# Reordering the opening of a two-block attention kernel: two issuing queues, inputs by pairs, weight splits four units later

## The reference

```python
# block 0, NH = 8 heads of 16 channels, x is (16, 128, 256), mask is (16, 256)
q = transpose(x) @ Wq.T                      # q serves as query, key and value
scores = 0.25 * einsum('bhqd,bhkd->bhqk', qh, qh)
logits = (scores * cmask + (1 - cmask) * -1e30) * rmask
x = x + transpose(softmax(logits) @ qh @ Wo.T)
# block 1: adaLN with cond (timestep_embed @ ada_w + ada_b), 16 heads of 128,
# x = x + gate1 * attention(ln(x)...),  x = x + gate2 * ffn(ln(x)...)
```

## Time and profile before

| | us |
|---|---|
| median of 3 runs | 842.45 (839.59 to 842.97) |
| the profiled execution, its time | 839.47 |
| its span, first to last instruction | 837.7 |
| PE busy | 778.3 (93%) |
| DVE busy | 389.4 (46%) |
| ACT busy | 434.5 (52%) |
| POOL busy | 144.7 (17%) |

### The profile page before, as it was taken

The page is one execution under the profiler, slowest core; times in us unless marked ns, Lnnn a source line. Parts: engine busy times, 40 slices in busy tenths (PEclk is TensorE's granted clock), DMA queues, the critical chain, the costliest instruction groups (busy, mean ns, idle before and its releaser), DMA issues. The chain is left out here.

```text
span 837.7 us, 13230 instructions
## 1 busy us (share of the span) xinstructions
PE 778.3 (93%) x4989; PEld 642.0 (77%) x4989; DVE 389.4 (46%) x782; ACT 434.5 (52%) x1189; POOL 144.7 (17%) x136
## 2 busy tenths in 40 slices
PE   4599999985999999999999999999999999799997
PEld 3455555553888888888888898888898888677775
DVE  1156666664234434444554443544543435436443
ACT  1056766663456544536555446465444475475553
POOL 3134343100222111101101011011011132200000
PEclk9999999997899999999999999999999999989999
DMA  6998999700311000000000000000000001030001
GB/s 197 242 167 195 194 188 199 124 8 32 108 39 38 1 1 1 1 2 1 1 1 1 0 0 0 0 0 0 1 2 1 13 27 38 13 101 27 15 10 50
DMA packets 26449, 42.64 MB, mean 51 GB/s; under 512 B 1960, under 2 KB 13728, under 8 KB 26400
## 3 DMA queue, kind: packets, MB, share of 16 engines
q1 hardware_dynamic: 26400, 41.98, 21.4%
HBM read 31.45 MB, written 10.52 MB: 50 GB/s over the span
## 5 line engine op out<-in xcount | busy, mean ns | idle before, releaser
L928 ACT ACTIVATE probs<-pair,nm 128x128 f32<-128x128 f32 x256 | 90.5, 366 | 218.0 <-DVE nm L1015 218.0
L1071 POOL TENSOR_TENSOR probs<-probs,rinv 128x512 f32<-128x512 f32 x64 | 66.6, 1041 | 391.4 <-DVE rinv L1024 391.4
L674 PE MATMUL bank<-x1h,w_hi 128*128 128x512 f32 x256 | 112.2, 438 | 5.0 <-DVE x1l L1001 5.0
L604 DVE TENSOR_REDUCE mx<-ring 128x2 fp32r<-128x512 f32 x128 | 80.1, 684 | 63.9 <-PE ring L403 63.9
L674 PE MATMUL bank<-x1h,w_lo 128*128 128x512 f32 x256 | 101.6, 397 | 0.0
L674 PE MATMUL bank<-x1l,w_hi 128*128 128x512 f32 x256 | 101.5, 397 | 0.0
L541 ACT ACTIVATE pt<-ring 128x512 f32<-128x512 f32 x128 | 70.0, 594 | 43.9 <-PE ring L415 43.9
L1045 DVE COPY Vv<-pair 128x512 f32<-128x512 f32 x64 | 44.3, 692 | 82.8 <-PE pair L674 82.8
L674 PE MATMUL pair<-w_hi,x1l 128*128 128x256 f32 x256 | 72.8, 284 | 0.0
L674 PE MATMUL pair<-w_lo,x1h 128*128 128x256 f32 x256 | 72.7, 284 | 0.0
L674 PE MATMUL pair<-w_hi,x1h 128*128 128x256 f32 x256 | 72.3, 282 | 0.0
(11 more groups left out here) (166 smaller groups left out, 1565.5 us busy)
## 6 DMA issues: line engine op xcount, KB each, us to landing
QS<-qd SPq DMA_DIRECT2D x16, 384.0 KB
stage<-in_L_cond_qkv_w_dram SPq DMA_DIRECT2D x12, 512.0 KB, 7.3
qd<-qh SPq DMA_DIRECT2D x16, 256.0 KB
KS<-qd SPq DMA_DIRECT2D x16, 256.0 KB
mb<-in_cond_dram SPq DMA_DIRECT2D x8, 256.0 KB, 10.2
qd<-ql SPq DMA_DIRECT2D x8, 256.0 KB
KS<-qd SPq DMA_DIRECT2D x16, 128.0 KB
kept<-X SPq DMA_DIRECT2D x1, 2048.0 KB, 8.0
```

The costliest lines, as they stand in the source:

```text
L604: dve.tensor_reduce(mx[:, 2 * b + s, :], ring[:, 2 * b + s, :].rearrange("p (k q) -> p k q", k=2), AX_X, ALU.max, negate=True).then_inc(dv ...
L674: last = nc.tensor.matmul(bank, w(k), x(k), start=(start and i == 0), stop=(stop and i == len(terms) - 1))
L928: last = nc.scalar.activation(probs[:, h % 2, b, :], Sb[:, b * T:(b + 1) * T], ACT.Exp, bias=nm[:, h % 2, b:b + 1], accum_out=sums[:, h % ...
L1071: pool.tensor_tensor(probs[:, h % 2, :, :], probs[:, h % 2, :, :], rinv[:, h % 2, :, None].to_broadcast([P, GB, T]), ALU.mult).then_inc(po ...
```

## The change

- **Two queues for the early loads.** SP keeps x and mask of group 0, Wq and the constants. ACT's stream now begins with eleven transfers: cond, Wo, x and mask of group 1, two of ada_w, and five biases.
- **x in pairs.** `pair(eng, g)` loads x and mask of one group; the single load of groups 2 to 7 goes away. SP issues pair(2) before the loop and pair(g+3) in it.
- **Mask rows first.** DVE makes `rows` in place of POOL; SP waits for their store and issues the four mask-row transfers ahead of gather(0). `spread` is cut in two functions, `mask_rows` and `spread`.
- **First spread in halves.** Group 0's q rows go as two sets of six transfers, for units 0 and 1, then 2 and 3; s(0) waits for the first set, s(2) for the second.
- **Splits four units later.** Half i of the weights is split in unit n = i + 4 on ACT and POOL. `weights(c)` and its wait are as they were.
- **Modulations first.** All four parts stand before the loop.

```diff
+    SPLIT0 = 4
...
-                def spread(g):
+                def mask_rows(g, landed):
...
-                sp.dma_start(X[:, 0:2, :], x[0:2].rearrange("b p d -> p b d")).then_inc(l_x0, 16)
-                mask(0)
+                pair(sp, 0)
                 sp.dma_start(wqo[:, 0, :], Wq).then_inc(l_w, 16)
                 sp.dma_start(cst[:, :], consts).then_inc(l_cst, 16)
...
-                sp.wait_ge(pool_nb, 1)
+                sp.wait_ge(dve_rows, 1)
                 sp.dma_start(rowd.rearrange("t b d -> b t d"), rows[:, :, :]).then_inc(l_nb, 16)
+                sp.wait_ge(l_nb, 16)
+                mask_rows(0, l_head)
                 gather(0)
...
-                sp.wait_ge(l_nb, 16)
-                spread(0)
-                sp.dma_start(X[:, 4:B, :], x[4:B].rearrange("b p d -> p b d")).then_inc(l_x, 16)
-                mask(2)
+                spread(0, slice(0, 2), l_head)
+                spread(0, slice(2, 4), l_q[0])
                 gather(1)
+                pool_free(2)
+                pair(sp, 2)
                 weights(0)
                 weights(1)
                 for g in range(NGR):
                     if g + 1 < NGR:
-                        spread(g + 1)
+                        mask_rows(g + 1, l_q[(g + 1) % 2])
+                        spread(g + 1, slice(0, 4), l_q[(g + 1) % 2])
                     if g + 3 < NGR:
-                        mask(g + 3)
+                        pool_free(g + 3)
+                        pair(sp, g + 3)
                     if g + 2 < NGR:
                         gather(g + 2)
...
-                    if n < 2 * CHUNKS:
-
-                        wait(pool, act_hi, n + 1)
...
+                    i = n - SPLIT0
+                    if 0 <= i < 2 * CHUNKS:
+
+                        wait(pool, act_hi, i + 1)
...
+                        if g == 0:
+                            pe.wait_ge(l_head, LQ)
+                        else:
+                            pe.wait_ge(l_q[g % 2], rows_in(g))
...
-                modulations(0)
-                modulations(1)
+                for part in range(4):
+                    modulations(part)
...
+                act.dma_start(cnd, cond).then_inc(l_cnd, 16)
+                act.dma_start(wqo[:, 1, :], Wo).then_inc(l_w, 16)
+                pair(act, 1)
+                for k in range(KT):
+                    act.dma_start(aw[k], ada_w[k * P:(k + 1) * P, :]).then_inc(l_ada, 16)
```

More of the change, by code:

```diff
@@ L215, in first_block @@
         aw = [late[:, 0:6 * DIM], pt[:, 1, :, :, :].rearrange("p a s n -> p (a s n)")[:, 0:6 * DIM]]
-        l_cst, l_small, l_w, l_x0, l_x1, l_x, l_ada = (sem(n) for n in (
-            "l_cst", "l_small", "l_w", "l_x0", "l_x1", "l_x", "l_ada"))
+        l_cst, l_small, l_w, l_ada = (sem(n) for n in ("l_cst", "l_small", "l_w", "l_ada"))
         l_mb = [sem("l_mb0"), sem("l_mb1")]
@@ L221, in first_block @@
         l_qd = [sem("l_qd0"), sem("l_qd1")]
-        l_nb, pool_nb = sem("l_nb"), sem("pool_nb")
+        l_nb, dve_rows, l_cnd, l_head = (sem(n) for n in ("l_nb", "dve_rows", "l_cnd", "l_head"))
+        l_xp = [sem("l_xp0"), sem("l_xp1")]
         qd = nc.dram_tensor("qd", (2, NH, 3, DK, 512), F32).ap()
@@ L236, in first_block, with pair, rows_in @@
         CHUNKS = QKV_COLS // CHUNK
+        def pair(eng, g):
+            src = cond[2 * g:2 * g + 2, :].rearrange("b d -> (b d)").partition_broadcast(P)
+            eng.dma_start(X[:, 2 * g:2 * g + 2, :], x[2 * g:2 * g + 2].rearrange("b p d -> p b d")).then_inc(l_xp[g % 2], 16)
+            eng.dma_start(mb[:, g % 2, :], src).then_inc(l_mb[g % 2], 16)
+        def rows_in(g):
+            return (6 * 16 if g % 2 == 0 else LQ) + LQ * (g // 2)
         def normal(b):
@@ L250, in _, with pool_free @@
             def _(sp):
[L251 to L255, removed]
+                def pool_free(g):
+                    sp.wait_ge(pool_x, g - 1)
                 def gather(g):
@@ L275, in spread @@
                             sp.dma_start(dst[r:r + 1, g % 2, :, :].bitcast(F32),
-                                         row[:, None, :].to_broadcast([1, 4, 512])).then_inc(l_q[g % 2], 16)
+                                         row[:, None, :].to_broadcast([1, 4, 512])).then_inc(landed, 16)
+                def spread(g, units, landed):
                     v = qd[g % 2].rearrange("(j s) c d n -> s (c d) j n", s=2)
@@ L281, in spread @@
                             r = 64 * s + r * DK
-                            sp.dma_start(dst[r:r + n * DK, g % 2, :, :].bitcast(F32),
-                                         v[s, DK * c:DK * (c + n)]).then_inc(l_q[g % 2], 16)
+                            sp.dma_start(dst[r:r + n * DK, g % 2, units, :].bitcast(F32),
+                                         v[s, DK * c:DK * (c + n), units]).then_inc(landed, 16)
                 def weights(c):
@@ L353, in _ @@
                         masked(n // 4 + 2)
-                    if n < 2 * CHUNKS:
-                        wait(pool, act_hi, n + 1)
-                        pool.tensor_tensor(w_lo[:, n * 512:(n + 1) * 512],
-                                           stage[:, n // 2 % 2, n % 2 * 512:n % 2 * 512 + 512],
-                                           w_hi[:, n * 512:(n + 1) * 512].bitcast(F32),
+                    i = n - SPLIT0
+                    if 0 <= i < 2 * CHUNKS:
+                        wait(pool, act_hi, i + 1)
+                        pool.tensor_tensor(w_lo[:, i * 512:(i + 1) * 512],
+                                           stage[:, i // 2 % 2, i % 2 * 512:i % 2 * 512 + 512],
+                                           w_hi[:, i * 512:(i + 1) * 512].bitcast(F32),
                                            ALU.subtract).then_inc(pool_lo, 1)
@@ L396, in scores @@
                     if j == 0 and b == 0:
-                        pe.wait_ge(l_q[g % 2], LQ * (g // 2 + 1))
+                        if g == 0:
+                            pe.wait_ge(l_head, LQ)
+                        else:
+                            pe.wait_ge(l_q[g % 2], rows_in(g))
+                    if g == 0 and j == 2 and b == 0:
+                        pe.wait_ge(l_q[0], rows_in(0))
                     wait(pe, act_exp, 4 * (n - 1) + 2 * b + 2)
@@ L434, in _ @@
                 pe.wait_ge(l_cst, 16)
-                pe.wait_ge(l_w, 48)
+                pe.wait_ge(l_w, 32)
+                pe.wait_ge(l_cnd, 16)
                 for i in range(2):
@@ L513, in _ @@
             def _(act):
+                act.dma_start(cnd, cond).then_inc(l_cnd, 16)
[3 more added lines that the diff above has]
+                    act.dma_start(aw[k], ada_w[k * P:(k + 1) * P, :]).then_inc(l_ada, 16)
+                row = 0
+                for src in (ada_b, out_b, ffn_b1, ffn_b2, qkv_b):
+                    n = src.shape[0] // P
+                    act.dma_start(bias_rows[row:row + n, :], src.rearrange("(n p) -> n p", p=P)).then_inc(l_small, 16)
+                    row += n
                 act.wait_ge(l_cst, 16)
@@ L572, in _ @@
                         values(n // 4 + 1)
[L573 to L576, removed]
+                    i = n - SPLIT0
+                    if 0 <= i < 2 * CHUNKS:
+                        wait(act, l_st[i // 2 % 2], 16 * (i // 4 + 1))
+                        nc.scalar.copy(w_hi[:, i * 512:(i + 1) * 512],
+                                       stage[:, i // 2 % 2, i % 2 * 512:i % 2 * 512 + 512]).then_inc(act_hi, 1)
                     if n < UNITS:
@@ L619, in modulated @@
                     dve.tensor_scalar(qb_s[:, :], qkvb[:, 0, :], SC, None, ALU.mult).then_inc(ada_done, 1)
+                dve.wait_ge(l_cnd, 16)
+                dve.tensor_copy(rows[:, 0, :], cnd)
+                dve.tensor_scalar(rows[:, 1, :], cnd, -NEG * DK ** 0.5, NEG * DK ** 0.5, ALU.mult,
+                                  ALU.add).then_inc(dve_rows, 1)
                 dve.wait_ge(pe_wT, 1)
```

22 lines of the change are left out of this document (2 added, 20 removed).

## The result

The changed kernel takes 921.54 us (median, 919.06 to 923.75) against 842.48 before: 1.0945 times as long, 95% interval 1.0908 to 1.0983. The forecast was 927, in a range of 898 to 948. The profiled execution took 923.75 us with a span of 921.2; before, 837.7. Its span is 83.5 us longer, and PE is 84.7 us late at s(28) already (257.83 against 173.12), so all of the loss arose in `first_block`.

What follows compares the result with a forecast made beforehand. Transfers matter only in `first_block`; the question was when PE reaches its 32 units. Opening -5.5, waits +79, clock +12.5, splits +0.9 make +86.9 on 839.5, or 926.4, forecast 927; own range 912 to 940, 8 in 10 898 to 948.

Steps and rivals of the forecast that it cites:

- The waits: PE at s(8), s(12), s(16), s(20), s(24) waits 15.8 us each for q rows held behind the later splits: +79 us.
- Rival 1: Same five places: waits are shorter, 12 us each, cold clock 2 each; 905 us in all. Chance 0.14.
- rival 3: spread(g+2) is not held before s(4g+8), so only the opening counts; 838 us. Chance 0.04.
- rival 2: Waits drag later work behind them, another 3 to 4 us per group, and s(28) waits too; 945 us. Chance 0.10.
- The opening: Start up to s(4): s(0) near 27.9, s(4) at 53.7 in place of 59.20; -5.5 us, bounds -9 and -2.
- rival 4: Opening gains nothing because ACT's late table load and ada_w transfers hold back gather(0); 5.5 us more, no separate chance.
- The clock: Behind each of the five waits PE runs at 1.2 GHz: 2.5 us each, bounds 0 to 4, +12.5 us.
- Splits in units 24 to 27: These units now carry splits: 19.24 - 18.30 = +0.9 us.

Runs made afterwards that it cites:

- experiment 1: The changed kernel with the splits back in units 0 to 23, all else as changed; 838.78 us, ratio 0.9998 to the kernel before.
- experiment 2: The kernel before with only the splits moved, to units 4 to 27; 925.37 us, ratio 1.1008.
- experiment 3: The changed kernel with the splits two units later in place of four; 871.84 us, ratio 1.0369.
- Experiment 6: The changed kernel with SP asking for chunk 2g, gather(g+2), then chunk 2g+1, and chunks 0 and 1 behind spread(1); 828.44 us, ratio 0.9866.
- Experiment 10: The changed kernel with 28 matmuls of constant data on PE ahead of each of the five waits; 923.84 us, in a second run 922.39.
- its second run: The changed kernel, unaltered, run again on the same chip as the second run with PE kept busy; 922.16 us, ratio 1.0980.
- the two runs with filler: Both runs of the changed kernel with 28 constant-data matmuls on PE ahead of each of the five waits; 923.84 and 922.39 us.
- Experiment 4: The changed kernel with SP asking for the chunks one step later, splits still four units later; 838.01 us, ratio 0.9977.
- experiment 7: The changed kernel with SP asking for chunk 2g, gather(g+2), then chunk 2g+1, and ACT's early transfers spread over the opening; 832.92 us, ratio 0.9917.
- experiment 8: Experiment 6 with ACT's early transfers spread over the opening as in experiment 7; 829.12 us, ratio 0.9870.

## Why the prediction was right, point by point

**The waits.** Forecast five of 15.8 us, at s(8), s(12), s(16), s(20), s(24), 79 us. Measured 16.09, 16.50, 15.38, 16.94 and 15.16, 80.1 us. The landing from the first q row was put at 12.7 and was 12.9 at s(8). Experiments 1 and 2 show the cause by removing it alone and by making it alone, and experiment 3 its size by the distance of the count. Rival 1 (12 us each) and rival 3 (no wait) are out, and so is rival 2: s(28) did not wait. What the prediction held against rival 1, that spread(0) took 12.4 us almost alone, was a wrong reading: 1.5 MB of x were issued at 20.91, in the middle of it, and the DMA share was 1.08 from 22 to 26 us. The size came out all the same. What made the term good was that the kernel before already ran the same queue order at the same place; the change only turned the 19 us of cover off.

**The opening.** Forecast -5.5 us at s(4), measured 53.04 - 59.20 = -6.2, which rules out rival 4 (the opening gains nothing). But several of its steps were off, and that they did not show in the end is partly luck. I had the first projection near 9.6 from ACT's issues and table load alone; it came at 10.46. What came last were the constants, which landed 6.0 us after their issue in place of 2.8, so that PE's transposes began at 8.21. gather(0) went out 1.5 us later than I said, and its last transfer landed near 20.4 in place of 17.8. That did not reach s(0), forecast 27.9 and measured 28.20, because PE's modulations ended last there, as the working had it. s(1) followed s(0) by 3.7 us, not 6, and PE was ready for s(4) at 48.57, not 51. That gained nothing here, because s(4) waited 4.47 us for spread(1): forecast 53.7, measured 53.04. Experiment 6 confirms that the rows' landing set it.

The Trainium skill, page DMA: Bandwidth & Descriptors, section Issuing engines are not separate DMA queues, says transfers of all issuing engines share the same DMA engines and that several issuers save only issue time. The trace agrees: x and mask of group 1, issued by ACT, and the constants, issued by SP, were under way together. Here the second queue even did harm in the first 8 us, since it put large transfers beside small ones that PE waited for (constants 6.0 us to landing, 2.8 before).

**The clock.** Forecast 2.5 us for each of the five waits, 12.5 in all; this term was mis-sized. The group that begins at s(8) takes 37.55 us, less the 16.50 of wait before s(12) 21.05, against 18.81 before: 2.2 more. The groups from s(12), s(16), s(20) and s(24) take 2.1, 1.1, 0.7 and 2.4 more, so the five are 8.6 us longer, 1.7 each. The group from s(4) is 2.2 longer too, behind its wait of 4.47 us, which the prediction did not count. Together that is 10.8. The windows behind s(8) in the changed kernel, answering to the earlier trace rows, show the clock at 0.50 and 0.56 and then back:

```profile
85.00:91.00 6.00, 0.39 (x4) 0.40 (x4) 0.00 (x0) 0.00 (x0) 0.00 (x0) 0.50 1.07 178
91.00:97.00 6.00, 6.00 (x30) 3.05 (x32) 2.08 (x4) 2.98 (x6) 4.39 (x4) 0.56 0.31 119
97.00:103.00 6.00, 5.62 (x52) 3.39 (x45) 4.71 (x10) 3.52 (x8) 1.29 (x1) 1.00 0.08 9
```

It costs one unit, not two: unit 8 takes 6.75 us against 4.42, unit 9 4.51, as before. My price came from the stretch 42.09 to 59.20, which also holds DVE's modulation arithmetic, as I had said.

Experiment 10 could not show that these microseconds are the clock's, but its rows and the changed kernel's can. Behind every wait PE is busy without a pause for 6 us, and the clock comes back sooner behind some waits than behind others. The 6 us from s(8) and from s(16) in the changed kernel:

```profile
90.61:96.61 6.00, 6.00 (x26) 3.24 (x26) 1.98 (x3) 2.59 (x6) 4.39 (x4) 0.53 0.36 139
164.61:170.61 6.00, 6.00 (x36) 3.18 (x38) 2.70 (x5) 3.17 (x6) 4.40 (x4) 0.72 0.41 155
```

With a granted clock of 0.53 unit 8 takes 6.75 us, with 0.72 unit 16 takes 5.81. All twenty such units, five each in the changed kernel, in its second run and in the two runs with filler, lie within 0.06 us of one straight line, from 6.95 us at 0.50 to 5.75 at 0.72. Drawn on to a clock of 1.00, it gives 4.43 us (an estimate), and the kernel before took 4.42 for unit 8. So nothing is left for another cause, such as operands of POOL or ACT that come late behind the wait. By the same line the five units of the changed kernel lost 10.0 us to the clock; the groups are only 8.6 longer, mostly because those of the kernel before lose about a microsecond to late chunks in these units.

The Trainium skill, page TensorE: Matmul & The Clock Gate, Part 1, says that for modeling "the ramp penalty is <1% of a typical kernel span". That was worth 8.4 us here. The 10.8 us that the groups lost besides their waits are 1.2% of the 921.2 us span, so this kernel lies above that figure: its penalty comes once behind each wait.

**The rest.** Splits in units 24 to 27: forecast +0.9, measured nothing. The group from s(24) is 2.4 us longer, but unit 24, behind the wait, takes all of it (6.84 us against 4.41); from s(25) to s(28) it is 13.87 against 13.89. Experiment 4, with splits in the same units and no wait, takes 18.30 from s(24) to s(28), as the kernel before does. The 19.24 that the forecast subtracted from is the group from s(4), and the other groups with splits take from 18.81 up, so the difference was not the splits' price.

The sum of the measured terms is -6.2 + 80.1 + 10.8 + 0 = 84.7 at s(28), where I had 86.9. The clock behind the five waits was forecast too high by 3.9 and the splits by 0.9; the opening was 0.7 better; the waits were 1.1 longer, and the 2.2 behind s(4) were not in the sum. So the mechanism held, and that the total is this near is in part that errors of the smaller terms cancelled.

The forecast of 927 is 5.5 us above the measured median: 2.65 from the sum (926.4 for the profiled execution, which took 923.75), 2.2 because this execution was above its median, and 0.6 from rounding up. The execution of the kernel before was 3.0 below its median, and the forecast did not add that in full. With it, it would have been 929.4. Median against median, the change costs 79.1 us, where the sum had 86.9.

## What to carry to other kernels

When a consumer is moved later, look for whoever waits for its count, and at what stands behind that wait in the same queue: here a buffer's reuse held the loads that the next group needed first. A wait on an in-order issuing queue is harmless only as long as everything behind it has slack, so move the request with the consumer. Experiment 6, in which the requests are moved and the first two chunks stand behind spread(1), is 1.3% faster than the kernel before, where the change had cost 9.4%. And put large early loads behind the small ones that start the work, whichever queue issues them; in experiment 7 that brought PE's first transposes 2.9 us forward, though the time did not fall by anything that can be measured; s(4) still waited 2.7 us for its rows there.

## What the runs showed of the hardware that was not expected

- A PE pause of 1.83 us, with the DMA engines at 0.93 busy, was followed by a granted clock of 0.50 for the next 4 us (experiment 4). A pause of 0.92 us at the same unit in experiment 1, for the same reason, was followed by scores of 0.50 us, that is full speed, and so was one of 1.38 us at s(20) in experiment 8.
- The clock fell right behind a gap of 2.99 us although PE had been busy with filler for 12 us before it (experiment 10, second run): it was 1.00 until 87.90, through the gap and the first matmuls of s(8), and 0.50 from 88.50.
- The constants, 68 KB, issued at 2.21 us, landed 6.0 us after their issue when ACT had 0.5 MB of x and mask and 1.5 MB of ada_w on their way, and 3.1 us after it when ACT issued those only once the constants had landed. Which of the two loads holds them up was not separated. The landing rows, first of the changed kernel and then of experiment 7:

```profile
cst<-stack_constants SPq DMA_DIRECT2D x1, 68.0 KB, 6.0
rowd<-rows SPq DMA_DIRECT2D x1, 32.0 KB, 7.2
```

```profile
cst<-stack_constants SPq DMA_DIRECT2D x1, 68.0 KB, 3.1
rowd<-rows SPq DMA_DIRECT2D x1, 32.0 KB, 1.6
```
